# GpSimd's order in a turn: the second low half of o, LayerNorm 2's root and the residual's bias; the residual's load first on the queue

## The reference

```python
q = relu((x @ Wq).reshape(b, s, 64, 64)) * SCALE
k = relu((x @ Wk).reshape(b, s, 64, 64))
v = (x @ Wv).reshape(b, s, 64, 64)
kv = einsum('bsid,bsjd->bsdj', k, v)
out = einsum('bsid,bsdj->bsij', q, kv)
q_norm = einsum('bsid,bsd->bsi', q, k.sum(axis=2))
out = (out / (q_norm[..., None] + EPS)).reshape(b, s, 4096)
x = layernorm(x + out @ Wo + bo)
gate, y = fp4_linear(x, w_gate), fp4_linear(x, w_up)
x = layernorm(x + fp4_linear(silu(gate) * y, w_down))
```

## Time and profile before

| | |
|---|---|
| median of 3 runs | 2255.24 us (2254.98 to 2257.67) |
| profiled execution | 2258.28 us, span 2256.5 us |
| PE busy | 2053.0 us (91%) |
| PE weight loads | 1958.4 us (87%) |
| DVE busy | 1809.7 us (80%) |
| POOL busy | 1727.8 us (77%) |
| ACT busy | 1601.0 us (71%) |
| DMA queue of the kernel | 302.65 MB, 62.4% of 16 engines |
| chain that ended last | PE 39%, DVE 31%, POOL 15%, ACT 7%, issue 5%, DMA 2% |

### The profile page before, as it was taken

One profiled execution on the slowest core, in us unless ns is written; L12 is line 12 of the kernel. 1 busy time (PEld: TensorE's weight loads), 2 busy tenths in 40 slices (PEclk: granted clock), 3 DMA queues, 4 the chain that ended last, 5 costly groups with the idle time before them and its releaser, 6 DMA issues.

```text
span 2256.5 us, 89008 instructions
## 1 busy us (share of the span) xinstructions
PE 2053.0 (91%) x37963; PEld 1958.4 (87%) x37963; DVE 1809.7 (80%) x3487; ACT 1601.0 (71%) x3210; POOL 1727.8 (77%) x2384
## 2 busy tenths in 40 slices
PE   4899999999999999999999999999999999999985
PEld 3798998998898898998898898898898899899874
DVE  6778878878878878888887887887887887887874
ACT  4677777777777777777777777777777777777762
POOL 4587787787787787787788778778778778778772
PEclk9899999999999999999999999999999999999986
DMA  6466666666666766756756766766766766666661
GB/s 195 100 137 145 142 134 138 149 128 138 149 131 135 151 132 135 157 126 136 154 129 133 154 132 131 155 133 130 151 135 130 149 138 131 146 142 130 141 130 34
DMA packets 523218, 308.34 MB, mean 137 GB/s; under 512 B 275590, under 2 KB 497734, under 8 KB 522310
## 3 DMA queue, kind: packets, MB, share of 16 engines
q1 hardware_dynamic: 522822, 302.65, 62.4%
HBM read 17.38 MB, written 4.19 MB: 10 GB/s over the span
## 4 chain that ended last, share of the span: by engine, by line
PE 39%; DVE 31%; POOL 15%; ACT 7%; issue 5%; DMA 2%; SPq 0%; DVEq 0%; POOLq 0%; ACTq 0%
PE ps L409 15%; DVE k_acc L775 9%; PE ps L362 8%; PE ps L364 8%; PE ps L363 8%; POOL q_nat L1082 7%; DVE v_st L793 5%; POOL o_st L1092 4%; DVE q L810 3%; ACT q_nat L609 3%; DVE k_acc L786 3%; ACT v_st L541 3%; DVE x L867 2%; DVE o L828 2%; POOL small L1100 2%
## 5 line engine op out<-in xcount | busy, mean ns | idle before, releaser
L1092 POOL TENSOR_TENSOR o_st<-o,o_st 128x256 bf16<-128x256 f32 x1024 | 663.2, 680 | 100.4 <-ACT o_st L651 100.4
L1082 POOL TENSOR_TENSOR q_nat<-q,q_nat 128x512 bf16<-128x512 f32 x512 | 589.4, 1174 | 32.1 <-ACT q_nat L609 31.1
L828 DVE TENSOR_TENSOR o<-ps,rec 128x512 f32<-128x512 f32 x512 | 354.2, 692 | 263.9 <-POOL o_st L1092 257.2
L362 PE MATMUL ps<-v_st,q_bd 128*128 128x66 bf16 x4096 | 457.0, 199 | 67.7 <-DVE o L828 62.0
L362 PEld LDWEIGHTS ps<-v_st,q_bd 128*128 128x128 bf16 x4096 | 420.1, 114 | 86.9 <-DVE o L828 69.4
L363 PE MATMUL ps<-v_st,q_bd 128*128 128x66 bf16 x4096 | 454.7, 198 | 0.0
L364 PE MATMUL ps<-v_st,q_bd 128*128 128x66 bf16 x4096 | 453.3, 197 | 0.0
L651 ACT CAST o_st<-o 128x256 bf16<-128x256 f32 x1024 | 357.6, 402 | 117.8 <-DVE o L828 112.7
L363 PEld LDWEIGHTS ps<-v_st,q_bd 128*128 128x128 bf16 x4096 | 417.6, 116 | 0.4 <-issue 0.4
L364 PEld LDWEIGHTS ps<-v_st,q_bd 128*128 128x128 bf16 x4096 | 417.0, 115 | 0.0
L409 PE MATMUL ps<-w_o,o_st 128*128 128x128 bf16 x6144 | 377.5, 220 | 5.2 <-DMA o_st<-swap 5.2
(11 more groups left out here) (130 smaller groups left out, 5413.6 us busy)
## 6 DMA issues: line engine op xcount, KB each, us to landing
q_bd<-q_nat SPq DMA_DIRECT2D x256, 256.0 KB, 3.9
swap<-v_st SPq DMA_DIRECT2D x64, 576.0 KB, 5.2
v_st<-v_st SPq DMA_DIRECT2D x64, 576.0 KB, 6.1
v_st<-swap SPq DMA_DIRECT2D x64, 576.0 KB, 6.6
swap<-o_st SPq DMA_DIRECT2D x64, 512.0 KB, 4.9
o_st<-o_st SPq DMA_DIRECT2D x64, 512.0 KB, 7.4
o_st<-swap SPq DMA_DIRECT2D x64, 512.0 KB, 6.0
x_in<-in_L_attn_x SPq DMA_DIRECT2D x64, 64.0 KB, 5.9
```

Source lines behind the costliest of these rows:

```text
L362: nc.tensor.matmul(dst, lhs(0), rhs(0), start=True, stop=False)
L828: nc.vector.tensor_tensor(o32[:, g % OR, :].rearrange("p (s b e) -> p s b e", b=2, e=HALF), slot_cols(("out", g))[:, :, 0:PW].rearrange("p ...
L1082: last = nc.gpsimd.tensor_tensor(qnat[:, 1, a, :, e, :], src[:, a], qnat[:, 0, a, :, e, :], ALU.subtract)
L1092: last = nc.gpsimd.tensor_tensor(lo[:, :, a], src[:, a], hi[:, :, a], ALU.subtract)
```

## The change

On SP the load of `x_res`, with its wait for `residual_1`, moves to the head of the turn, ahead of the moves of q's low half. On POOL the bias `x_bias` moves from behind `rstd_2` to ahead of `x_back`, and `o_lo(1)` moves ahead of `rstd_2`. No instruction is added or removed, and the other engines' lists stay.

```diff
             def iteration(t):
+                if t.mid:
+                    if t.back:
+                        sp.wait_ge(s_r1, t.b + 1)
+                    sp.dma_start(x_res[:, :], x_t[bass.ts(t.m, T), :]).then_inc(s_xres, 16)
                 if t.attend:
                     sp.wait_ge(s_qlo, (t.n * NC))
                     q_move(1, 0)
...
                     move(v4[t.par], vsw, s_vswap, vm[0], 0)
-                if t.mid:
-                    if t.back:
-                        sp.wait_ge(s_r1, t.b + 1)
-                    sp.dma_start(x_res[:, :], x_t[bass.ts(t.m, T), :]).then_inc(s_xres, 16)
                 if t.mid:
                     move(o4[t.par], osw, s_oswap, om[1], 1)
...
                 q_stay(t)
+                x_bias(t)
                 x_back(t)
                 o_lo(t, 0)
                 q_lo(t, 0)
+                o_lo(t, 1)
                 rstd_2(t)
-                x_bias(t)
-                o_lo(t, 1)
                 q_lo(t, 1)
                 o_lo(t, 2)
                 o_lo(t, 3)
```

## The result

The changed kernel takes 2305.04 us in the median of four runs (2302.83 to 2305.41), against 2255.11 us for the kernel before in the same session: a ratio of 1.0217, interval 1.0199 to 1.0235. It is 50 us slower; 39 us slower was forecast. The profiled execution took 2305.13 us with a span of 2303.3 us (2256.5 before).

What follows compares the result with a forecast made beforehand. It took a loop over several engines, with POOL lacking slack from `q_lo(0)` to `q_stay`, as the bound. Sixty turns each 0.65 us longer add 39 to 2258.3, giving 2297; less 3.0 for the median, 2294; range 2268 to 2338.

Steps and rivals of the forecast that it cites:

- The load: Load of `x_res` on SP, moved ahead of q's low-half moves: counted at nothing; 40 us if its cover failed.
- If it blocked a DVE step: Danger for `x_bias` on POOL beside DVE: blocking a step for its whole length costs 0.45 a turn, 27 us.
- The bias: `x_bias` on POOL leaves the loop, 0.41 us, and costs nothing in the 4.8 us where POOL waits for DVE.
- q_lo(1) late by 1.27: On POOL, `q_lo(1)` starts at 1061.60 in place of 1060.33, as later nb delays `y` and `q_hi(1)` on ACT.
- some 1.7: POOL's forecast idle time in us ahead of `q_lo(1)`, while it waits for ACT's `q_hi(1)`.
- The way to the next turn: Delay followed from POOL over ACT, DVE and PE to the next `k_add(2)`: of 1.27 us, 0.65 reaches the turn.
- Rival B: `x_scale` on DVE held until the last `q_stay` copy ends, `k_add(2)` late by 1.27: 76 us, 2331; chance 0.22.
- margin of 0.24 us: Forecast room between `x_scale`'s start at 1046.9 and the third `q_stay` copy's end at 1047.14, against steps good to 0.1.
- rival C: Faster: `y` on ACT does not hold `q_hi(1)` back, 0.41 gained in 62 turns, 25 us, 2230; chance 0.13.
- POOL's loop sets the turn: POOL is part of the loop setting the 33.64 us turn, without slack between `q_lo(0)` and `q_stay`.
- its hold at `x_scale`: POOL's `q_stay` holds DVE's `x_scale`, 0.55 us where 0.155 was seen elsewhere; `k_add(2)` follows.
- C's second price, 2194: Time in rival C if the lock between DVE and POOL slipped too and PE's wait of 0.98 us were gained.

Runs made afterwards that it cites:

- `y` alone: Kernel before with only `y` moved behind `q_hi(1)` on ACT: 2253.26 us, ratio 0.9988.
- The bias alone: Kernel before with `x_bias` ahead of `x_back` and its load first on the queue, the root still ahead of `o_lo(1)`: 2226.86 us, ratio 0.9863.

## Why the prediction was right, and where it was not

**The load** was counted at nothing, and is: 0.9996 by itself. Its landing was put at 5.2 us and took 2.0 in the new place. That the new place is worth 11 us to the bias was not foreseen: by a landing of 5.2 us the load is in at 1051.0 in its old place, in time for `x_back` at 1051.7. What costs there is that the bias runs beside DVE's chain, which the prediction had named as a danger ("If it blocked a DVE step") and priced at 0.45 a turn; it was 0.26 in 35 turns.

**The bias** was counted at nothing in its new place; it runs there right behind `q_stay` with no wait. In the changed kernel it brings nothing, as said: POOL's 1.27 was counted with the 0.41 taken off.

**q_lo(1) late by 1.27** was measured as 1.28 (the root has four instructions, not the five of the prediction, which took its length from the rows and so lost nothing by it), POOL's idle of "some 1.7" as 1.70, ACT's wait of 1.6 as 1.59. The order of ACT's steps is the cause, shown from both sides: `o_lo(1)` ahead of the root alone gives the whole cost (2305.8), and `y` one step further back turns it into a gain (2200.5).

**The way to the next turn.** From `q_lo(0)`, `scale_o(5)` was put at 11.47 us (1066.53 - 1055.06) and came at 11.46 (1017.48), `q_hi(3)` at 13.34 and came at 13.31, `q_stay_next` at 14.66 and came at 14.64, `v_lo(0)` at 18.84 and came at 18.83. `k_add(2)`, the last step, was put at 1047.48 + 33.64 - 1055.06 = 26.06 and came at 26.13. So the turn is longer by 0.74 where 0.65 was forecast, 5 us of the 11 that were missing. 0.07 of the 0.09 lies in PE's k chunk 2, the rest in the reading of the steps.

**Rival B** was treated as one or the other, with a margin of 0.24 us. It was both: the margin came out at 0.03, `x_scale` wins in 50 turns and loses in ten. That adds 4 us. Its price in a turn is 0.44, not the 1.27 - 0.65 = 0.62 of the prediction, because the copies ended about 0.1 earlier than summed and `k_add(2)` came later by PE in any case. The first turns gain 1.8 where nothing was counted. The rest, about 3 us, is the difference between profiled executions and medians (before, the profiled one lay 3 us above its median; after, at it). The Trainium skill, SBUF — State Buffer, section Who interferes with whom, says that issue order decides who blocks; the starts at 1031.62 and at 1066.02 agree with it.

**What fell** is a part of the account of the kernel before, and the first price of rival C. That POOL's loop sets the turn before stands: `y` alone and the table show it. But the prediction put its hold at `x_scale`, and that one is worth only 0.10 us, with PE right behind it. The hold that counts is on `x_one`, 0.94 us in place of 0.34, which the prediction does not name; both together make 0.5 a turn. Rival C had "the lock keeps DVE behind POOL, so 0.41 is the gain", 25 us. The lock did not keep. In the changed kernel with `y` moved `scale_o(3)` and with it PE come earlier by more than POOL does, `x_one` gets ahead of the copy, and the gain was 57 us. C's second price, 2194, is within 7 us of what was measured, in part by luck: it stands for PE's 0.98, and the 0.97 of the trace is 0.46 of POOL and 0.51 of the hold.

The bias alone got 0.50 us a turn in the same way: its `q_lo(1)` is where it was, the holds are gone (20.14 to 19.63). The forecast did not rest on `x_one`, since it followed the steps of the changed kernel over ACT and PE. It had the 1.27 shrink to 0.65 on that way; measured, 1.29 shrinks to 0.74, and the 0.55 between them is the hold that the changed kernel no longer has.

## What to carry to other kernels

An instruction that looks free to be put off (four small ones here) has a reader, and what counts is what is queued behind that reader on its engine: look for a wait that is already there, as `y`'s 0.3 us was. A move that is a loss can be half of a gain; the other half is the reader's place in its own list. Of two paths that are equal within 0.1 us the profile shows both as busy without a gap, and only an edit that moves one of them tells which sets the time. An edit that changes nothing can still hide a move: look whether an instruction has become longer, as `x_one` did when POOL came earlier.

## What the runs showed of the hardware that was not expected

- The hold between DVE and POOL is decided by 0.03 us of start time and makes turns of two lengths, 34.38 and 34.82, in one execution.
- The hold of `x_one` makes one and the same instruction last 0.34 or 0.94 us: 0.94 when it starts 0.25 us behind a copy of 1.04 us on POOL, ending 0.15 behind it, and 0.34 when it starts 0.17 ahead.
- It works in both directions: a bias on POOL of 0.46 us took 1.16 beside DVE's steps with two inputs in SBUF, and where the bias was first a step of DVE of 0.29 took 0.55. This was seen in a trace and not tried by itself.
- Halving an instruction on POOL does not halve it: 64x512 elements took 1.04 us and 64x256 took 0.62 (from 500 to 2000 us, medians of 1042 and 622 ns).
- The load of `x_res`, 64 KB, lands in 5.0 us among the swaps and in 2.0 at the head of the turn (medians of the issues at both places):

```profile
DMA to landing us min/median/max: 1.7/2.0/3.8
```
